# A graph layer on one core: normalised node rows go to DRAM and are gathered from there by edge groups 16 to 48, and two pieces of the node step come later in it

## The reference

```python
h = relu(layer_norm(x))                                   # no gain or bias
em = concat([h[src], h[dst]]) @ msg_w + msg_b             # per edge
em = relu(layer_norm(em) * msg_g + msg_beta) * edge_weight
messages = segment_sum(em, dst) / counts                  # 0 where there are none
gate = sigmoid(h @ gate_w + gate_b)
h_new = relu(layer_norm(concat([h, messages]) @ upd_w + upd_b) * upd_g + upd_beta)
out = x + gate * h_new + (1 - gate) * h
```

## Time and profile before

| | us |
|---|---|
| median of 3 runs (909.29 to 910.00) | 909.52 |
| the profiled execution, its own time | 908.32 |
| its span, first to last instruction | 906.6 |

### The profile page before, as it was taken

The page is one execution under the profiler, slowest core; times in us unless marked ns, Lnnn a source line. Parts: engine busy times, 40 slices in busy tenths (PEclk is TensorE's granted clock), DMA queues, the critical chain, the costliest instruction groups (busy, mean ns, idle before and its releaser), DMA issues.

```text
span 906.6 us, 20426 instructions
## 1 busy us (share of the span) xinstructions
PE 664.2 (73%) x4448; PEld 530.6 (59%) x4448; DVE 847.5 (93%) x3820; ACT 834.8 (92%) x3476; POOL 608.9 (67%) x602
## 2 busy tenths in 40 slices
PE   1877777877777777768578778777787787877871
PEld 0555555655555556555466667666676676666760
DVE  6799999999999999999998999999999999999994
ACT  2799999999999999999789999999999999999972
POOL 4777776666666666666557777657776666664467
PEclk9999999899999999999869998999989999899885
DMA  5355555556556566555223232332211211211111
GB/s 152 97 177 168 175 166 172 162 174 194 177 179 185 182 179 187 176 184 162 73 68 101 66 105 84 103 100 81 83 63 62 70 58 64 71 52 55 58 63 34
DMA packets 60436, 107.96 MB, mean 119 GB/s; under 512 B 14566, under 2 KB 16438, under 8 KB 60370
## 3 DMA queue, kind: packets, MB, share of 16 engines
q1 hardware_dynamic: 39756, 71.88, 23.7%
q0 software_dynamic: 18912, 34.84, 14.4%
q10 hardware_dynamic: 1702, 0.53, 0.3%
HBM read 56.01 MB, written 55.12 MB: 123 GB/s over the span
## 4 chain that ended last, share of the span: by engine, by line
ACT 44%; DVE 36%; issue 10%; PE 4%; POOL 3%; DVEq 1%; ACTq 1%; DMA 1%; POOLq 0%
ACT junk L402 11%; DVE work L752 9%; DVE work L454 9%; ACT hrow L395 9%; ACT xload L395 7%; DVE st L353 6%; ACT work L433 6%; POOL out L607 3%; DVE mv L359 3%; ACT at L1069 2%; ACT work L1126 2%; ACT work L1124 2%; DVE work L731 2%; ACT lnv L377 2%; DVE e L444 2%
## 5 line engine op out<-in xcount | busy, mean ns | idle before, releaser
L607 POOL DMA_INDIRECT out<-work,sidx x196 | 201.7, 1029 | 121.9 <-issue 57.6
L602 POOL DMA_INDIRECT ring<-in_x,src_i x196 | 205.0, 1046 | 79.0 <-issue 54.6
L602 POOL DMA_INDIRECT ring<-in_x,gidx x140 | 142.1, 1015 | 51.0 <-issue 39.0
L395 ACT ACTIVATE hrow<-xload,nb,rs 128x128 f32<-128x128 f32 x392 | 164.4, 530 | 1.6 <-DVE nb L388 1.6
L402 ACT ACTIVATE junk<-py 128x128 bf16<-128x128 f32 x588 | 155.2, 296 | 1.0 <-PE py L1289 1.0
L402 ACT ACTIVATION_READ_ACCUMULATOR junk<-py 128x1 f32 x588 | 133.6, 230 | 0.0
L1203 PE MATMUL pa<-ident,work 128*128 128x128 f32 x376 | 62.6, 290 | 92.6 <-DVE work L731 92.4
L1245 PE MATMUL py<-w_u,work 128*128 128x129 f32 x784 | 119.6, 298 | 0.0
L1245 PEld LDWEIGHTS py<-w_u,work 128*128 128x128 f32 x784 | 99.9, 200 | 21.8 <-issue 21.8
L1203 PE MATMUL pt<-ident,hrow 128*128 128x128 f32 x588 | 101.6, 301 | 13.1 <-ACT hrow L395 12.9
L454 DVE SCALAR_TENSOR_TENSOR work<-hrow,omg,xload 128x128 f32<-128x128 f32 x392 | 108.5, 338 | 0.0
(11 more groups left out here) (170 smaller groups left out, 1832.6 us busy)
## 6 DMA issues: line engine op xcount, KB each, us to landing
xload<-in_x SPq DMA_DIRECT2D x98, 256.0 KB
out<-work SPq DMA_DIRECT2D x98, 256.0 KB
running_sums<-acc SPq DMA_DIRECT2D x49, 256.0 KB, 2.1
staged_target_rows<-work SPq DMA_DIRECT2D x14, 256.0 KB, 3.6
ring<-staged_target_rows SPq DMA_DIRECT2D x14, 256.0 KB, 3.1
ring<-in_x,src_i POOLq DMA_INDIRECT x196, 3.0
out<-work,sidx POOLq DMA_INDIRECT x196, 2.2
ring<-in_x,gidx POOLq DMA_INDIRECT x140
```

The lines of the kernel that those rows point to most:

```text
L395: last = nc.scalar.activation(dest[:, m, :], rows[:, m, :], ACT.Relu, bias=nb[:, s4, at + m:at + m + 1], scale=rs[:, s4, at + m:at + m + 1])
L602: pool.indirect_dma_start(out=dest, out_offset=None, in_=rows, in_offset=bass.IndirectOffsetOnAxis(ap=idx, axis=0), **(if_tail if rows is ...
L607: pool.indirect_dma_start(out=out, out_offset=bass.IndirectOffsetOnAxis(ap=idx, axis=0), in_=rows, in_offset=None, **if_tail).then_inc(s, 16)
```

## The change

Each normalised row group `hrow` of the node phase is also stored to a DRAM tensor `normalised_rows` by SP, four steps behind (98 stores of 256 KB), and ScalarE waits for the store of g-4 before it overwrites the buffer. The edge groups 0 to 15 are as before. The edge groups from LATE = 16 on gather their source rows from that tensor: they need no statistics, no moments and no ReLU for the source half, and TensorE transposes them from `ring` itself, waiting for the gather. Their gathers can't stand beside the node steps: after the node loop GpSimd waits for all stores and gathers UPFRONT = 12 groups (16 to 27) at once; the source rows of groups 28 to 48 are refills, 96 in all with the 12 target gathers, over the same 36 groups. In the node step VectorE's `node_sum` moves from the start of the step to behind the `bn_stats`, and ScalarE's evacuation of `pt` moves behind the squares (`node_post`). The load of `bias3` is issued ahead of x load 4 instead of after x load 7.

```diff
@@ -52,7 +52,8 @@
 WIDE = 96
 RING = 32
 EARLY = 5
-AHEAD = 7
+LATE = 16
+UPFRONT = 12
 REFILLED = 36
 STAGED = 14
 DIRECT = EG - STAGED
@@ -166,6 +167,9 @@
+        h_dram = nc.dram_tensor("normalised_rows", (N, H), f32).ap()
@@ -359,34 +364,38 @@
+        def late(g):
+            return g.at >= LATE
         def moment(L, g, n, which):
-            v = st[:, g.at % 4, 0:n, :]
+            s4, a = (g.at + 1) % 4, G if late(g) else 0
+            v = st[:, g.at % 4, a:n, :]
...
-        def logs(act, d, s, k, scale=1.0):
+        def logs(act, d, s, k, scale=1.0, a=0):
-        def rstds(act, d, s, k):
+        def rstds(act, d, s, k, a=0):
-        def minus_mean(dve, d, g, n, factor=-1.0):
+        def minus_mean(dve, d, g, n, factor=-1.0, a=0):
@@ -514,6 +523,12 @@
                         q = g.back(1)
                         sp.wait_ge(s_st[q.at % 4], q.rounds(16, 16))
                     sp.dma_start(rows(out, g), o[:, g.at % 4]).then_inc(s_st[g.at % 4], 16)
+                q = s.back(4)
+                if live(q, NG):
+                    nd["h"].after(sp, q)
+                    if q.turn is None and q.at == NG - 1:
+                        sp.wait_ge(s_hst[(q.at - 1) % 4], q.back(1).rounds(16, 16))
+                    sp.dma_start(rows(h_dram, q), hrow[:, q.at % 4]).then_inc(s_hst[q.at % 4], 16)
                 if s.turn is not None and s.at in (lead + 1, lead + 5):
                     i = (s.at - lead) // 4
@@ -525,9 +540,10 @@
             edge_column(src_i, src, s_e, 2)
             edge_column(w_f, edge_weight, s_e, 3)
             for g in range(1, XS):
+                if g == 4:
+                    sp.wait_ge(s_bsplit, 1)
+                    sp.dma_start(bias3[:, :], bias_b[0:1, :, :]).then_inc(s_b3, 16)
                 node_step(Group(g))
-            sp.wait_ge(s_bsplit, 1)
-            sp.dma_start(bias3[:, :], bias_b[0:1, :, :]).then_inc(s_b3, 16)
             run_steps(sp, node_step, NG, XS, lead, 8, first=XS)
@@ -554,6 +570,7 @@
             for i in range(4):
                 sp.wait_ge(s_st[i], 16 * len(range(i, NG, 4)))
+                sp.wait_ge(s_hst[i], 16 * len(range(i, NG, 4)))
                 sp.wait_ge(s_sums[i], 16 * len(range(i, EG, 4)))
                 sp.wait_ge(s_scat[i], 16 * G * len(range(i, EG, 4)))
             sp.wait_ge(s_to, 16)
@@ -601,7 +618,7 @@
             def gather(dest, rows, idx, s):
                 pool.indirect_dma_start(out=dest, out_offset=None, in_=rows,
                                         in_offset=bass.IndirectOffsetOnAxis(ap=idx, axis=0),
-                                        **(if_tail if rows is x else {})).then_inc(s, 16)
+                                        **({} if rows is sums_dram else if_tail)).then_inc(s, 16)
             def scatter(rows, idx, s):
                 pool.indirect_dma_start(out=out, out_offset=bass.IndirectOffsetOnAxis(ap=idx, axis=0),
@@ -611,7 +628,7 @@
                 if k == 0 and g >= 4:
                     pool.wait_ge(s_gsrc[g % 4], G * 16 * (g // 4))
                 c = g * G + k
-                gather(slot(Group(g), 0)[:, k, :], x, src_i[:, c:c + 1], s_gsrc[g % 4])
+                gather(slot(Group(g), 0)[:, k, :], h_dram if g >= LATE else x, src_i[:, c:c + 1], s_gsrc[g % 4])
             def gather_dst(g, k):
                 if k == 0 and g >= 4:
@@ -626,7 +643,7 @@
                     gather_src(g, k)
             pool.wait_ge(s_prep, TARGETS)
             prefetch = [(part, g, k) for g in range(RING)
-                        for part in ((gather_dst,) if g < EARLY else (gather_src, gather_dst)) for k in range(G)]
+                        for part in ((gather_src, gather_dst) if EARLY <= g < LATE else (gather_dst,)) for k in range(G)]
             total, done, bounced = len(prefetch) + STAGED * G, 0, 0
             for g in range(NG):
                 if 30 <= g < 30 + 4 * STAGED:
@@ -644,12 +661,13 @@
                 nd["mix"].after(pool, Group(g))
             assert done == len(prefetch) and bounced == STAGED * G
-            for g in range(AHEAD):
-                ed["h"].after(pool, Group(g), 1)
+            for i in range(4):
+                pool.wait_ge(s_hst[i], 16 * len(range(i, NG, 4)))
+            for g in range(LATE, LATE + UPFRONT):
                 for k in range(G):
-                    gather_src(g + RING, k)
-            refills = [(part, g, k) for g in range(RING, EG)
-                       for part in (((gather_src,) if g >= RING + AHEAD else ()) + ((gather_dst,) if g < DIRECT else ()))
+                    gather_src(g, k)
+            refills = [(part, g, k) for g in range(LATE + UPFRONT, EG)
+                       for part in ((gather_src,) + ((gather_dst,) if RING <= g < DIRECT else ()))
                        for k in range(G)]
             for i in range(4):
                 pool.wait_ge(s_st[i], 16 * len(range(i, NG, 4)))
@@ -667,11 +685,11 @@
                     scatter(o[:, g % 4, k, :], sidx[:, c:c + 1], s_scat[g % 4])
                 upto = min(len(refills), (g + 1) * len(refills) // REFILLED + 1)
                 for part, q, k in refills[refilled:upto]:
-                    if k == 0 and part is gather_src:
-                        ed["h"].after(pool, Group(q - RING), 1)
-                    elif k == 0:
+                    if k == 0 and q >= RING and part is gather_src:
+                        ed["flip"].after(pool, Group(q - RING), 1)
+                    elif k == 0 and q >= RING:
                         ed["mix"].after(pool, Group(q - RING))
-                    assert q - RING <= g + (AHEAD if part is gather_src else 0)
+                    assert q - RING <= g + (5 if part is gather_src else 0)
                     part(q, k)
                 refilled = upto
                 if g == TAIL_SLOT:
@@ -718,6 +736,8 @@
                 if new:
                     L.begin(dve, s)
                     L.mark(row_stats(L, s, xload[:, s.at % XS, 2:4], 2))
+                if between is not None:
+                    between(s)
                 if live(s.back(1), NG) and (s.turn is not None or s.at > 1):
                     minus_mean(dve, nd, s.back(1), G)
                 if new:
@@ -756,8 +776,7 @@
                     final(dve, nc.vector, nd, f, o[:, f.at % 4])
             def node_step(s):
-                node_sum(s)
-                node_rows(s)
+                node_rows(s, node_sum)
             def border_columns():
@@ -912,11 +931,12 @@
                 if drained and s.at <= EG + 2:
                     early = mix_early(early + 1)
                 if new:
-                    dve.wait_ge(s_gsrc[s.at % 4], s.rounds(G * 16, G * 16))
                     L = ed["stats"]
-                    row_stats(L, s, slot(s, 0), 0)
+                    if not late(s):
+                        dve.wait_ge(s_gsrc[s.at % 4], s.rounds(G * 16, G * 16))
+                        row_stats(L, s, slot(s, 0), 0)
                 if live(s.back(1), EG):
-                    minus_mean(dve, ed, s.back(1), 2 * G, -0.5)
+                    minus_mean(dve, ed, s.back(1), 2 * G, -0.5, G if late(s.back(1)) else 0)
                 q = s.back(3)
                 if live(q, EG):
                     if beyond(q, 4):
@@ -1084,16 +1104,18 @@
                 if live(s.back(5), NG):
                     turned_relu(s.back(5))
                 rstds(act, nd, s, 2 * G)
+                node_post(s)
                 g = s.back(2)
                 if live(g, NG):
                     evacuate(nd, g, ht_dst[:, g.at % 4, :], pt[:, g.at % 2, :], ACT.Copy, "ht", "flip")
-                node_post(s)
                 node_h(s)
             def node_h(s):
                 g = s.back(1)
                 if live(g, NG):
                     nd["nb"].after(act, g)
+                    if beyond(g, 4):
+                        act.wait_ge(s_hst[g.at % 4], g.rounds(16))
                     one_mark(nd["h"], act, g, h_rows(g, hrow[:, g.at % 4], xload[:, g.at % XS], 0))
             def node_post(s):
@@ -1107,8 +1129,9 @@
                     ed["post"].after(act, s.back(7))
                 if live(s.back(3), EG):
                     ed["square_m"].after(act, s.back(3))
-                logs(act, ed, s, 4 * G, 1.0 / H)
-                rstds(act, ed, s, 4 * G)
+                a = G if late(s.back(1)) else 0
+                logs(act, ed, s, 4 * G, 1.0 / H, a)
+                rstds(act, ed, s, 4 * G, a)
                 if node is not None and live(node.back(4), NG):
                     if live(node.back(1), NG):
                         nd["stats"].after(act, node.back(1))
@@ -1142,13 +1165,19 @@
                     ed["nb"].after(act, g)
                     H_ = ed["h"]
                     H_.begin(act, g)
-                    H_.mark(h_rows(g, hrow[:, (g.at + NG) % 4], slot(g, 0), 0))
+                    if late(g):
+                        H_.mark(h_rows(g, h_dst[:, (g.at + NG) % XS, 0:2], slot(g, 1)[:, 0:2], G))
+                    else:
+                        if g.at < 4:
```

(44 more changed lines are left out.)

## The result

The changed kernel takes 916.14 us (915.72 to 916.70, 4 runs) beside 909.76 for the kernel before in the same runs: a ratio of 1.0066, 95% interval [1.0049, 1.0084]. The forecast was 926.2. The sign and the mechanism of the edge phase were right; the forecast's 16.7 us more were 2.6 times what came out, because the node phase gained 25.3 us and not 13.

What follows compares the result with a forecast made beforehand. GpSimd's indirect-DMA queue was taken to bound the edge phase: 463.5 + 68.2 + 330.2 + 72.9 + 1.5 = 936.3, less 13 for node steps, 923.3 span, plus 1.7 and 1.2: 926.2 us, range 903 to 946.

Steps and rivals of the forecast that it cites:

- GpSimd's queue as the bound: Edge phase: 343 indirect DMAs from the last node wait at 463.54 set the time; VectorE held some 9 us in step 11.
- The pitch: GpSimd's time per indirect DMA in the edge phase: 1.42 us up front, 1.37 in the paced part, 1.35 in the tail.
- The node step: Node loop: two moves shorten a step from 4.31 to 4.17 us, 13 us in all; bounds 0 and 15 us.
- the ScalarE floor: Node step: ScalarE's evacuation no longer waits for TensorE's flip, 4.31 less 0.15 to 0.18, about 4.15 us.
- the moved bias load at nothing: First 30 us: the bias load ahead of x load 4 costs nothing, since loads are issued steps ahead of use.
- "Booked at nothing" for the lighter edge steps: Edge groups 16 to 48: less VectorE and ScalarE work, up to 26 us, counted as nothing because GpSimd's queue paces them.
- Rival 3: Edge phase: VectorE, not GpSimd, is the bound; 870 us, needing a pitch of 1.21; chance 0.03.
- The stores at nothing: Node loop: the 98 stores of h cost nothing, DMA share 0.75; bound of 20 us if a load is late.
- Rival 1: Edge phase: GpSimd keeps a 1.30 us pitch, 900 us, faster by 1%; decided at mean pitch 1.325; chance 0.17.
- Rival 4: Edge phase: VectorE's ops with two SBUF inputs hold up GpSimd, 61 us more, 987 us; chance 0.03.

Runs made afterwards that it cites:

- few_b: Changed kernel with one of four source parts gathered in groups 16 to 48, TensorE transposing that part four times; 842.74 us, ratio 0.9285.
- the row of borders: Changed kernel with LATE at 16, 24 and 32 (12, 8 and 7 groups up front): 916.14, 878.04 and 862.88 us.
- n_vec: Kernel before with only VectorE's `node_sum` moved behind the statistics; 886.92 us, ratio 0.9736.
- n_act: Kernel before with only ScalarE's evacuation of `pt` moved behind the squares; 906.55 us, ratio 0.9954.
- n_both_st: Kernel before with both node-step moves, the stores of h that nothing reads and the earlier `bias3` load; 883.22 us, ratio 0.9704.
- late32_b: Changed kernel with LATE = 32 instead of 16 and 7 groups up front instead of 12; 862.88 us, ratio 0.9492 to the kernel before.
- late24_b: Changed kernel with LATE = 24 instead of 16 and 8 groups up front instead of 12; 878.04 us, ratio 0.9646 to the kernel before.
- n_both: Kernel before with both moves of the node step and nothing else; 884.83 us, ratio 0.9715.

## Why the prediction was right in kind and off in size

**GpSimd's queue as the bound: right.** The count of 343, the last node wait as its start, no idle time, VectorE held some 9 us in step 11 (8.72) and steps of 9.2 us after it all came out. `few_b` and the row of borders show it by experiment and not by the trace alone.

**The pitch: right, 3 us off, and in part by luck.** I worked with 1.42, 1.37 and 1.35 for the up-front gathers, the paced part and the tail, 1.374 over all. They were 1.426, 1.380 and 1.358, over all 1.383: 343 x 0.009 = 3 us more. The 1.37 was the middle between two rows, chosen because I couldn't tell which DMAs would be lengthened; nothing in the working made it better than 1.33 or 1.41.

**The node step: the term that was mis-sized.** I gave it "0.14 x some 92 steps = 13 us"; the node phase ended 25.3 us earlier. That error of 12.3 us is what made the forecast's change 2.6 times too large. The step of the sum that failed is "4.31 - 0.16 = 4.15" on VectorE, rounded to 4.17, and the ScalarE floor beside it; the step came out at 4.06. I took the idle time in the brackets (0.16) for what the wait costs. From start to start `nb` to L731 was 0.31 us, and the same pair stands 0.12 apart with nothing to wait for, so that wait cost 0.19. The remaining 0.07 are the gate operations among the statistics: from the first of them (L444, at 215.55 in the row below) to `nb` it was 1.05 us, and from L453 to L772 in the changed kernel the same ones take 0.98. Together 0.26.

```profile
215.55 0.28 DVE L444 TENSOR_SCALAR e<-ge 128x4 f32<-128x4 f32 x1
```

The steps ahead of the loop, which had 4.05 us in the kernel before already (the row pair of 44.35 and 48.41), were a better gauge than the idle column: they show the step without the wait. I didn't look there. On ScalarE I counted 0.19 between two small operations where 0.11 was possible, and called 4.15 "the same floor": that was wrong as a reading, since `n_vec` and `n_act` show that ScalarE was not the bound. Of the 25.3 us the 84 steps of the loop between `nb` of groups 9 and 93 are 21.9 and the last four 0.6. The other 2.8 arise ahead of that, 2.6 of them before the loop (`nb` of group 8 at 52.46 and 49.88), where I had put the moved bias load at nothing; the kernels above point to it for some 2 of them, and it was not run alone.

Put together: 926.2 - 12.3 (node) + 3 (pitch) - 0.8 (what lies around the span, 2.1 us and not 2.9) = 916.1.

**"Booked at nothing" for the lighter edge steps: right, with a wrong price beside it.** The kernel as changed gets none of it: 916.1 us where `few_b`, with the same instructions on the other engines, has 842.7. Rival 3 had it at 0.8 us a group; it is 1.19.

**The stores at nothing: right** (`n_both_st`), at a DMA share of 0.75 in the node loop as worked out.

**The rivals.** Rival 1 had the gain of the node step too small by as much, and so its decision point at 1.325; with 25.3 us it is (906.6 - 465.0 + 25.3)/343 = 1.361. The measured 1.383 lies only 0.022 from it. That is why 0.75 for slower was too sure for what I knew of the pitch, whose own range began at 1.30. Rival 4 I threw out with one row, the node gather of 213.15 that ran through the `mix` rows. That row shows only that a DMA under way isn't held; one that starts inside such an instruction is. The rule of the Trainium skill (SBUF — State Buffer, section "Who interferes with whom") that a VectorE instruction with two SBUF inputs contends with a GpSimd instruction that reads SBUF holds in that form: the trace agrees at L484, L489 and L962, and L474, which reads PSUM, holds nothing (0.99 in some 45 cases). The same section of the Trainium skill reports that a `tensor_tensor` did not stall a DMA in its probe; here the indirect DMAs are held by one (L484, 1.25 us on average). What it costs was already in the 1.43 of the earlier trace rows, so the sum had it without the reason, at a chance of 0.03 for the reason that, by the estimate above, decides the sign. The 61 us that I gave it were the run time of the instructions, not the part of it that a start falls in.

## What to carry to other kernels

Count the instructions of the slowest-issuing queue phase by phase and multiply by their pitch, not by their busy time: work that moves from a phase where a queue has slack to one where it has little is not moved for free, even if it makes the visible bound lighter. Price a wait from start to start against the same pair without a wait, not by the idle column. Where two engines seem to stand at the same floor, move one alone before calling both the bound; and a border like LATE wants to be set so that neither queue waits long for the other. Of the three that were run `late32_b` is the best, 5% below the kernel before on this chip; its GpSimd still idles 38 us and that of `late24_b` not at all, and no border between 24 and 32 was run.

## What the hardware showed that I had not expected

- A GpSimd indirect DMA (0.98 us) that starts while VectorE runs an instruction with two SBUF inputs is lengthened until about 0.60 us after that instruction's start, if that is one of 128x512 (1.33 for the start at 702.27, 1.54 at the most in the rows above). Two such instructions back to back hold it through both (2.00 us at 452.47). One under way is not lengthened (0.99 in 28 cases).
- ScalarE's recorded durations are not its cost. In the gapless node loop of the changed kernel a copy of 128x512 is recorded with 1.15 us and a run of four ReLU rows with 2.19, in the kernel before with 0.60 and 1.67; from start to start the first takes 0.47 and the second 1.54 in both, near enough. A stretch without gaps is not what makes the record longer: `n_vec` has none either and records the copy with 0.69, `n_both` with 1.15, so it comes with ScalarE's move on top of VectorE's. Why is open.
- In `n_both_st` 81% of the DMA engines' time (257 GB/s) in the node loop left VectorE and ScalarE without a gap (197.00 of 197.00 us).
